# Attention with a second, transposed score product in place of transposed probabilities

## The reference

```python
q = _layer_norm(query, ln1_g, ln1_b)
qh = (q @ wq + bq).reshape(Bq, Sq, H, hd)
kh = (context @ wk + bk).reshape(Bq, Sc, H, hd)
vh = (context @ wv + bv).reshape(Bq, Sc, H, hd)
scores = jnp.einsum('bqhd,bkhd->bhqk', qh, kh) * scale
allowed = pos_in_block[None, :] <= jnp.arange(Sq)[:, None]
scores = jnp.where(allowed[None, None, :, :], scores, NEG_INF)
probs = jax.nn.softmax(scores, axis=-1)
o = jnp.einsum('bhqk,bkhd->bqhd', probs, vh).reshape(Bq, Sq, Dm)
x = query + o @ wo + bo
```

## Time and profile before

| | |
|---|---|
| Time, median of three executions | 2956.3 us |
| Profiled execution | 2956.78 us |
| Its span, mean granted TensorE clock | 2955.1 us, 0.989 |
| TensorE, VectorE, ScalarE, GpSimd busy in the span | 2786.7, 2033.4, 1654.5, 355.2 us |

### The profile page before, as it was taken

How to read it: one execution, slowest core, us unless ns; L and a number is a source line. 1 busy time by engine, 2 the same in 40 slices (tenths; PEclk the granted TensorE clock), 3 DMA queues, 4 the chain that set the end, 5 groups by cost and what they waited for, 6 DMA issues and landing times. The chain is left out here.

```text
span 2955.1 us, 65575 instructions
## 1 busy us (share of the span) xinstructions
PE 2786.7 (94%) x22056; PEld 2510.5 (85%) x22056; DVE 2033.4 (69%) x4884; ACT 1654.5 (56%) x4014; POOL 355.2 (12%) x364
## 2 busy tenths in 40 slices
PE   6999999999999999999984999999999899999999
PEld 4777777787777877777764999999999899999999
DVE  4766676667776677666756877877787766665566
ACT  3655666566655666566644565556556544444444
POOL 1211222112221122212210000000000000000000
PEclk9999999999999999999997999999999999999999
DMA  6666666667665676666634344334435343333442
GB/s 139 112 116 108 111 110 121 114 106 110 118 121 99 114 110 122 115 100 121 98 64 150 136 170 184 135 142 185 170 123 219 135 156 142 142 142 122 155 156 93
DMA packets 151738, 383.03 MB, mean 130 GB/s; under 512 B 12160, under 2 KB 16256, under 8 KB 143488
## 3 DMA queue, kind: packets, MB, share of 16 engines
q1 hardware_dynamic: 151680, 382.28, 52.8%
HBM read 172.51 MB, written 109.05 MB: 95 GB/s over the span
## 5 line engine op out<-in xcount | busy, mean ns | idle before, releaser
L711 ACT ACTIVATE sm<-sm,mins 128x128 f32<-128x128 f32 (+3 forms) x1024 | 571.6, 559 | 570.5 <-DVE mins L574 567.9
L574 DVE CUSTOM_DVE_ANT_0 sm<-bank_s,mask 128x128 f32<-128x128 f32 (+3 forms) x1024 | 480.6, 488 | 418.5 <-PE bank_s L425 416.2
L437 PE MATMUL bank_t<-ident,sm 128*128 128x128 f32 x2560 | 418.8, 278 | 73.8 <-DVE pT L520 37.4
L437 PEld LDWEIGHTS bank_t<-ident,sm 128*128 128x128 f32 x2560 | 299.6, 141 | 178.3 <-issue 58.3
L425 PE MATMUL bank_s<-stack 96*128 96x128 f32 (+3 forms) x1024 | 353.0, 386 | 8.4 <-DMA stack<-st_lo 7.9
L520 DVE COPY pT<-bank_t 128x384 f32<-128x384 f32 (+1 forms) x576 | 326.8, 567 | 1.3 <-PE bank_t L437 1.3
L1092 PE MATMUL bank_x<-b_hi,w_hi 128*128 128x256 f32 x1024 | 296.8, 290 | 26.9 <-ACT g L1515 21.6
L1092 PE MATMUL bank_x<-w_hi,a_hi 128*128 128x256 f32 x1024 | 291.2, 284 | 4.0 <-DVE a_lo L1212 4.0
L1093 PE MATMUL bank_x<-b_lo,w_hi 128*128 128x256 f32 x1024 | 291.1, 284 | 0.0
L1094 PE MATMUL bank_x<-b_hi,w_lo 128*128 128x256 f32 x1024 | 291.1, 284 | 0.0
L1094 PE MATMUL bank_x<-w_hi,a_lo 128*128 128x256 f32 x1024 | 290.9, 284 | 0.0
(11 more groups left out here) (178 smaller groups left out, 7389.4 us busy)
## 6 DMA issues: line engine op xcount, KB each, us to landing
stack<-st_hi SPq DMA_DIRECT2D x256, 256.0 KB, 6.1
xt<-in_x SPq DMA_DIRECT2D x32, 1024.0 KB, 5.1
stack<-st_lo SPq DMA_DIRECT2D x128, 256.0 KB, 7.3
xr<-x_scratch SPq DMA_DIRECT2D x32, 1024.0 KB, 5.6
b_scratch<-b_hi SPq DMA_DIRECT2D x16, 1792.0 KB, 10.0
b_scratch<-b_lo SPq DMA_DIRECT2D x16, 1792.0 KB, 13.7
b_hi<-b_scratch SPq DMA_DIRECT2D x16, 1792.0 KB, 7.5
b_lo<-b_scratch SPq DMA_DIRECT2D x16, 1792.0 KB, 11.2
```

Of the source, the lines that this page charges most:

```text
L437: mm = pe.transpose(bank_t[n % 2][:, P * c:P * c + P], sm[:, n % SLOTS_S, P * c:P * c + P], ident[:])
L574: op = V.tensor_tensor_reduce(sm[:, n % SLOTS_S, off:off + w], bank_s[n % BANKS_S][:, off:off + w], mask[:, 512 - w:512], 1.0, 0.0, ALU.ad ...
L711: op = A.activation(row, row, ACT.Exp, bias=mins[:, g % 2, c:c + 1], scale=-1.0, accum_out=sums[:, g % 2, c:c + 1])
```

## The change

Scores are computed twice. The first product is as before, but VectorE now writes its masked tile away as bf16 into `junk`, and only the minima are kept. Two-column products with the identity lay the minima of two heads as rows 96 and 97 of a PSUM bank (`minima_rows`); ScalarE copies them, negated and repeated for both heads, into rows 96 and 97 of `stack` (`minima_out`). Rows 96 and 97 of the key side hold ones and zeros that pick the head. The second product (`score_t`) then runs over 98 rows, with keys on partitions, and gives negated score less minimum, transposed. ScalarE takes the exponential from PSUM straight into `pT`, without a bias and without sums. GpSimd clears the masked half of the diagonal blocks (`mask_probs`) and adds the key tiles (`add_keys`). Job R becomes a product of those sums with ones, and VectorE takes the reciprocal of 128x512. `expand`, `r_copy`, `move_tile` and `p_transpose` are gone.

A group now has 20 steps: first scores in steps 0 to 11, second scores and exponentials of heads 0 and 1 in steps 9 to 11 and of heads 2 and 3 in steps 14 to 16, the V product in step 6 of the next group. BESIDE is laid out anew. ScalarE takes over the high part of the next context. In the start-up the order of a few operations on VectorE, ScalarE and TensorE is changed.

```diff
-SLOTS_S = 4
-LAG = 3
+SLOTS_S = 2
+BANKS_P = 2
+SCORES = [(r, qts) for p in (0, 2) for r, qts in
+          ((p, (0, 1)), (p + 1, (0, 1)), (p, (2,)), (p, (3,)), (p + 1, (2,)), (p + 1, (3,)))]
+MINIMA_AT = (7, 12)
+PROBS_AT = ((9, 10, 11), (14, 15, 16))
+PROBS = [(0, (0,)), (1, (0,)), (0, (1,)), (1, (1,)), (0, (2, 3)), (1, (2, 3))]
+KEY_AT = (0, 512, 896, 1152)
-    TG = 12
+    TG = 20
+    Q_AT, K_AT = {0: 4, 1: 4, 2: 4}, {3: 4, 4: 4, 5: 4}
     BESIDE = [
...
+        [("B", {0: 4}), ("Q1", Q_AT), ("K1", K_AT), ("R", {8: 8}), ("V1a", {9: 6, 10: 6, 11: 6, 12: 6}), ("O0", {14: 6, 15: 6}), ("O1", {16: 6, 17: 6})],
+        [("Q2", Q_AT), ("K2", K_AT), ("O2", {6: 6, 7: 6}), ("R", {8: 8}), ("V0b", {9: 6, 10: 6, 11: 6, 12: 6}), ("O3", {13: 6, 14: 6})],
+        [("Q3", Q_AT), ("K3", K_AT), ("V1b", {6: 8, 7: 8, 8: 8}), ("R", {8: 8}), ("X0", {15: 4}), ("X1", {16: 4}), ("X2", {17: 4}), ("X3", {18: 4})],
+        [("Q0", Q_AT), ("K0", K_AT), ("R", {8: 8}), ("V0a", {9: 6, 10: 6, 11: 6, 12: 6})],
     ]
+    PV_AT, RECIP_AT, O_PROD_AT, O_HIGH_AT, O_HIGH_LATE = 6, 9, 10, 11, 16
+    STATS_AT, NORMALISE_AT = (8, 9, 10, 11), (13, 13, 14, 14)
+    CONTEXT_AT = ((2, 9), (3, 1))
...
                 elif kind == "R":
-                    pe.wait_ge(rexp_ok, it.b * NG + g)
-                    for c in range(QT):
-                        mm = pe.transpose(bank[:, P * c:P * c + P],
-                                          rT[:, P * c:P * c + P], ident[:])
+                    pe.wait_ge(pre_ok, 2 * ADDS * (it.b * NG + g))
+                    for cols, src in ((slice(0, P), pT[:, :, 0:P]), (slice(P, 512), pre[:, :, :])):
+                        for h in range(4):
+                            mm = pe.matmul(bank[32 * h:32 * h + 32, cols], ones[:], src[:, h, :],
+                                           start=True, stop=True, skip_group_check=True)
...
+            def minima_rows(it, g, p):
+                n = PG * g + PG // 2 * p
+                pe.wait_ge(masked, it.b * TB + (SG * g + SG // 2 * (p + 1) + BANKS_S))
+                pe.wait_ge(scored_t_read, it.b * (NG * PG) + (n + 1))
+                for qt in range(QT):
+                    mm = pe.matmul(bank_p[n % BANKS_P][96:98, P * qt:P * qt + P], mins[:, g % 2, qt, 2 * p:2 * p + 2],
+                                   ident[:], start=True, stop=True, skip_group_check=True)
+                mm.then_inc(scored_t, 1)
+
+            def score_t(it, g, p, i):
+                n = PG * g + PG // 2 * p + 1 + i
+                pe.wait_ge(scored_t_read, it.b * (NG * PG) + (n + 1 + (i == 0)))
+                head, tiles = PROBS[i]
+                off = 0
+                for j in tiles:
+                    w = S - P * j
+                    mm = pe.matmul(bank_p[n % BANKS_P][:, off:off + w], stack[0:98, g % 2, 1, 2 * p + head, P * j:P * j + P],
+                                   stack[0:98, g % 2, 0, 2 * p + head, P * j:S], start=True, stop=True)
+                    off += w
+                mm.then_inc(scored_t, 1)
...
             def body(it):
                 for n, steps in enumerate(it.steps):
                     g, k = divmod(n, TG)
+                    if not it.tail and k < SG:
+                        score(it, g, k)
+                    for p in range(2):
+                        if not it.tail and k in PROBS_AT[p]:
+                            at = 2 * PROBS_AT[p].index(k)
+                            score_t(it, g, p, at)
+                            score_t(it, g, p, at + 1)
                     for job, i, j in steps:
                         dense_step(it, job, g, i, j)
+                    for p in range(2):
+                        if not it.tail and k == MINIMA_AT[p]:
+                            minima_rows(it, g, p)
+                    if k == PV_AT and not (it.first and g == 0):
+                        pv(it, g - 1)
...
+            def o_reciprocal(it, g):
+                bank = it.bank("R", g + 1)
+                dve.wait_ge(dense, it.done("R", g + 1))
+                dve.wait_ge(oT_done, it.b * NG + (g + 1))
+                V.reciprocal(rT[:], bank_d[bank][:]).then_inc(d_free[bank], 1)
...
+            def minima_out(it, g, p):
+                n = PG * g + PG // 2 * p
+                act.wait_ge(scored_t, it.b * (NG * PG) + (n + 1))
+                A.activation(stack[96:98, g % 2, 0, 2 * p:2 * p + 2, :],
+                             bank_p[n % BANKS_P][96:98, :].unsqueeze(1).to_broadcast([2, 2, S]),
+                             ACT.Identity, scale=-1.0).then_inc(scored_t_read, 1)
+
+            def exponential(it, g, p, i):
+                n = PG * g + PG // 2 * p + 1 + i
...
+                act.wait_ge(scored_t, it.b * (NG * PG) + (n + 1))
+                head, tiles = PROBS[i]
+                w = sum(S - P * j for j in tiles)
+                A.activation(pT[:, 2 * p + head, KEY_AT[tiles[0]]:KEY_AT[tiles[0]] + w], bank_p[n % BANKS_P][:, 0:w],
+                             ACT.Exp, scale=-1.0).then_inc(scored_t_read, 1)
...
+            def mask_probs(it, g, p):
+                n = PG * g + PG // 2 * p + 1
+                for j in range(QT):
...
+                    diagonal = pT[:, 2 * p:2 * p + 2, KEY_AT[j]:KEY_AT[j] + P]
+                    G_.affine_select(out=diagonal, in_=diagonal, compare_op=ALU.is_ge, fill=0.0, base=0,
+                                     pattern=[[0, 2], [1, P]], channel_multiplier=-1).then_inc(probs, 1)
+
+            def add_keys(it, g, p):
...
+                heads = slice(2 * p, 2 * p + 2)
+                G_.tensor_tensor(out=pre[:, heads, :], in0=pT[:, heads, P:S], in1=pT[:, heads, 512:896],
+                                 op=ALU.add).then_inc(pre_ok, 1)
+                for i, j in ((1, 2), (2, 3)):
+                    cols = slice(P * i, 384)
...
+                    G_.tensor_tensor(out=pre[:, heads, cols], in0=pre[:, heads, cols],
+                                     in1=pT[:, heads, KEY_AT[j]:KEY_AT[j] + S - P * j], op=ALU.add).then_inc(pre_ok, 1)
```

More of the change, by code:

```diff
@@ L627, in body @@
                     g, k = divmod(n, TG)
-                    if not it.tail:
-                        mask_and_max(it, n)
+                    if not it.tail and k < SG:
+                        mask_and_min(it, g, k)
                     for job, jg in it.ended(n):
@@ L632, in body @@
                             x_low(it, job, jg, it.b + 1)
[L633 to L634 removed]
                     beside_previous = g < NG and not (it.first and g == 0) and n < len(it.steps)
[L636 to L639 removed]
+                    if k == RECIP_AT and beside_previous:
+                        o_reciprocal(it, g - 1)
                     if k == O_PROD_AT and beside_previous:
@@ L741, in _ @@
             v_copy(pro, "V0a", 0)
+            act.wait_ge(consts, 1)
+            for par in range(2):
+                for p in range(2):
+                    A.copy(stack[96:98, par, 1, 2 * p:2 * p + 2, :],
+                           ident[96:98, 96:98].unsqueeze(2).to_broadcast([2, 2, S])).then_inc(chosen, 1)
             def body(it):
@@ L748, in body @@
                             x_high(it, job, jg)
-                    if not it.tail:
-                        exponential(it, n)
-                    if (n > LAG and not it.tail or n <= LAG and not it.first) and act_moves((n - LAG - 1) % TG):
-                        move_tile(act, A.copy, it, n - LAG - 1)
+                    for p in range(2):
+                        if not it.tail and k == MINIMA_AT[p]:
+                            minima_out(it, g, p)
+                        if not it.tail and k in PROBS_AT[p]:
+                            at = 2 * PROBS_AT[p].index(k)
+                            exponential(it, g, p, at)
+                            exponential(it, g, p, at + 1)
                     if not (it.first and g == 0):
-                        if k == R_AT:
-                            r_copy(it, g - 1)
                         if k == (O_HIGH_LATE if g == 1 else O_HIGH_AT):
                             o_high(it, g - 1)
+                    if not it.last and not it.tail:
+                        for half, at in enumerate(CONTEXT_AT):
+                            if (g, k) == at:
+                                for fb in (2 * half, 2 * half + 1):
+                                    context_high(it, it.b + 1, fb)
                     for job, jg in it.ended(n):
@@ L792, in o_low, with residual @@
+            def residual(b):
+                pool.wait_ge(res_in, b * 16 + 16)
+                for t in range(QT):
+                    G_.tensor_tensor(out=xt[:, t, :], in0=xt[:, t, :], in1=bo_row[:],
+                                     op=ALU.add).then_inc(res_ok, 1)
             def o_low(it, g):
```

261 lines of the change are left out of this document (106 added, 155 removed), and 4 rows, old and new, of the table BESIDE.

## The result

The changed kernel takes 3370.8 us (median, 3370.2 to 3371.8), the kernel before 2956.3 us beside it: a ratio of 1.141 [1.139, 1.143]. The forecast was 3207, with a range of 3020 to 3340. Sign and mechanism held, the size did not: +415 us where +251 were forecast.

The account below looks back on a forecast made before the run. TensorE was taken as the bound: 89.5 us of work plus 19.4 of waits made 108.9 a batch, +15.7, by 16 batches +251; last batch -6, tail +5. 2956.8 + 250 = 3207 us, range 3020 to 3340.

Parts of the forecast that it names:

- A: The forecast itself: whole kernel, TensorE's added work plus the new waits, 3207 us; chance 0.60.
- Rival C: TensorE runs its queue nearly dense once the copies go, waits 1.5 us a batch: faster, 2921 us; chance 0.08.
- B: Added latency hides in dense work, waits stay at 8.3 us a batch, only work grows: 3030 us; chance 0.15.
- Work, 89.5 us: TensorE's summed work in one batch of the attention stage at full clock: 89.5 us, 4.6 more than before.
- Step 12: Second pair's minima rows wait for VectorE's mask behind the reciprocal: nothing in groups 0, 1, 3; 1.9 us in group 2.
- Rival D: VectorE's 512-element reciprocal takes 4.2 us, delaying mask and minima rows 1.9 us in all four groups: 3329 us; chance 0.12.
- The clock at 1.00: TensorE in the attention stage: all 89.5 us of work a batch priced at full clock.
- rival E: TensorE's clock falls with gaps up to 3 us; 9 us of work a batch at half clock: 3351 us; chance 0.05.
- Steps 9 to 11, 14 to 16 and Q0: TensorE's waits for six exponentials twice a group, and Q0 of group 3 for X3: 3.7 + 6.4 + 2.6 us a batch.
- the old 8.3: Waits and gaps in the earlier kernel's 93.24 us batch, 8.3 us, forecast to go with the transpositions.
- Steps 12 to 14: Minima rows to ScalarE's copy to second score: 1.55 us without work beside in groups 0, 2, 3; 4.8 in all.
- GpSimd at nothing: GpSimd's adds (3.8 us) and four selects (2.6) per pair of heads cost TensorE no wait; doubled, up to 2 us a group.

Follow-up runs that it names:

- experiment 7: Changed kernel in 14-step groups, second-half minima, scores and exponentials beside the next group's Q and K; transposed minima, casts behind exponentials: 3093.6 us, 1.047.
- 11: The kernel of experiment 7 with 28 idle products a batch in its longest waits: 3060.0 us, 1.035.
- experiment 1: Changed kernel with a plain copy in place of VectorE's 128x512 reciprocal, the division left out: 3257.3 us, 1.102.
- experiment 2: Changed kernel with 57 idle 512-column products a batch put in TensorE's waits: 3296.2 us, 1.115.
- experiment 3: Changed kernel with GpSimd's adds in group 2 held until VectorE has normalised the next x: 3371.4 us, 1.141.
- experiment 9: The kernel of experiment 7 with statistics and O jobs a step earlier, inverse root ahead of GpSimd's adds, K0 earlier: 3103.8 us, 1.050.
- experiment 12: The kernel of experiment 7 with 15 idle products a batch and a copy in place of the reciprocal, division left out: 3023.4 us, 1.026.
- experiment 5: Changed kernel with minima laid as rows by four transpositions in place of four float32 products: 3322.2 us, 1.124.

## Why the prediction was wrong

The likeliest case was A. Of its steps:

- **Bound and sign: right.** TensorE is the bound, gets more work, and waits where there is no dense work beside. Rival C (faster) fell: the waits are 18 us a batch, not 1.5. B fell for the same reason; experiments 7 and 11 show how much of it would have been there with another order (a batch of 99.1).
- **Work, 89.5 us: 91.4.** The sums (0.94 forecast, 1.00 measured) and the V product (2.3) came as forecast. The minima rows did not: 0.27 us a product against 0.215, 8.6 us a batch instead of 6.9, which is 27 us in all. The price of the product was right, since the records of one set of four products start 0.109 us apart, 0.218 for the two of a product. What the sum left out is some 0.1 us at each end of a set: four products take 0.97 us from start to the next (649.42 to 650.39), and the one ahead of them is 0.09 longer. Two more terms were off by 2 us each and cancel: second scores at full clock take 1.39 us a pair of heads (0.47 + 0.51 + 0.41, 652.10 to 655.32), 11.1 a batch instead of 9.3, and first scores 3.0 a group (group 1), 12.0 a batch instead of 14.1.
- **Step 12, "nothing in groups 0, 1, 3", 1.9 us in group 2: this failed.** Measured 1.23 in each of the three and 3.48 in group 2, 7.2 a batch. The term that was mis-sized is the reciprocal: 2.3 us forecast from start to start, 3.27 measured (record 3.35). The mistake can be located in the earlier trace rows: I took 0.09 us of the 16-element pitch of 0.16 as fixed, by the neighbouring read. With 3.27 us for 512 elements and 0.16 for 16, it is 6.3 ns an element and some 0.06 fixed. A difference of two small numbers was carried on by a factor of 32. The queue behind it (masks, then minima rows) was counted correctly, and experiment 1 confirms it: with a short operation the wait stands in group 2 alone, 0.9 us. By the forecast's own rule 0.97 us more in four groups is 62 us, 3.9 a batch of the 5.3 by which these waits exceed the 1.9. The rest is TensorE, which reaches the rows earlier than walked: 5.2 us behind the end of the sums in group 0 where 5.5 was counted, 4.2 in group 2 where 4.85 was. Rival D had the right mechanism and too high a price: 8 passes at the mask's rate would be 8.1 ns an element, the Trainium skill's repeat count taken literally ("VectorE: DVE Perf Modes", "First, the fixed hardware budget"); the trace has 6.3.
- **The clock at 1.00: this failed too.** The sum priced all work at full clock, and rival E, at 0.05, had 9 us of work a batch at half clock. It was 13.38 + 6.67 us of busy records, which would be 10 us at full clock, close to E's 9. The row that I set against E, 25 of 35 us busy at 1.00, is an average over a stretch; it said nothing on how its idle time was divided. That stretch was 71% busy at 1.00, the changed kernel's batch is 87% busy at 0.89, so the share over a long stretch does not tell the clock. What stands around it is visible. The records date the fall at 594.7, just as the 3.48 us wait begins; TensorE had waited 0.29 and 0.74 us before it. Four more waits follow (1.11, 0.26, 1.07, 1.21) up to 611.0, and the clock is back at 615.2, after 4.2 us of Q0's products and scores without a wait. The second stretch, 635.7 to 642.5, is dense itself (6.7 us busy of 6.8); waits of 1.24, 1.11 and 0.45 us end 4, 2 and 1 us ahead of it. The Trainium skill warned of this ("TensorE: Matmul & The Clock Gate", "HAM oscillation"), and the trace agrees: the low clock comes back with each group 2. That idle time brings it is shown by experiment 2, which puts products in the waits and has 3.4 us at half clock instead of 27.3; it prices the clock at 75 us at least. Which of the waits it takes is open.
- **Steps 9 to 11, 14 to 16 and Q0, 3.7 + 6.4 + 2.6 us: over-sized.** Measured 3.2 us for exponentials and 1.2 ahead of Q0. In steps 9 to 11 of group 2, still at full clock, 0.29 + 0.74 us were lost where 2.8 stood in the sum; in its steps 14 to 16, at half clock, 0.26 + 1.07 for 3.3. That slower work of TensorE's own covers more of the round trips there is argued, not shown. With gaps, the waits sum to 18.1 against 19.4, so the total was nearly right by a short term and long ones. It is luck also because the forecast let all of the old 8.3 go with the transpositions, though the earlier trace rows has 5.1 of it ahead of them: the changed kernel has 3.0 us of gaps beside its 15.1 of idle time.
- **Steps 12 to 14, minima round trip, 1.55 us three times: right in kind.** 1.11 us of idle three times on the wait table, group 1 covered by O3, ScalarE's copy 1.02 us (1.1 forecast).
- **GpSimd at nothing: right for this kernel.** In a steady batch it is not named among TensorE's waits. The adds take 3.8 us a pair of heads, as forecast, the four selects 1.6 instead of 2.6. That it slows VectorE's normalisation was not foreseen; experiment 3 shows that it cost nothing. In experiment 9 GpSimd's place in the queue did cost 3.9 us.

The miss is 119.5 - 108.9 = 10.6 us a batch: work +1.9, clock +10.0, waits -1.3. Cases A, D and E stood as alternatives in the list, but they are not exclusive. A longer reciprocal lengthens a wait, and longer waits bring the clock down: A with 62 us for the reciprocal, 27 for minima rows and 75 for the clock comes to 3371 us, which is what was measured. That closeness is luck: experiment 2 gives only the lower end of the clock, and the over-sized and missing terms named above happen to cancel. The range ended at 3340 because D and E were each priced alone. It should have reached to their sum.

What stays open is the exact price of the clock alone (4.7 to 10.0 us a batch). The last 2.6% of experiment 12 have no single cause that was isolated. Not tried was the new order with a cheaper division, such as the old one on 128x16.

## What to carry to other kernels

Before trading a small operation for the same one on a large tile, find its price an element from two sizes; one short record here gave 4.4 ns for 6.3. An operation that stands ahead of a mask or a minimum in VectorE's queue can be paid for by TensorE. When a forecast adds waits of several us next to each other, price the work behind them at half clock too, and add the cases instead of listing them as alternatives. In this kernel the second stage of dependent work was better placed beside the next group's dense work than behind its own: of 415 us lost, moving it gave back 228 (experiment 7 less the 49 of experiment 5), a copy for the reciprocal 114 and holding the clock 75 (a run of its own each; the three overlap).

## What the runs showed of the hardware

- A reciprocal of 128x512 float32 on VectorE takes 3.35 us (3.27 from start to start), a copy of the same tile 0.69 (experiment 1).
- VectorE's float32 scalar operation from SBUF to SBUF takes 0.54 us alone and 0.98 to 2.04 while GpSimd adds or subtracts tiles of SBUF. The Trainium skill, "SBUF — State Buffer", "Who interferes with whom", has the two share a port pair that one holds for a whole instruction; the trace agrees in that each record of one batch's four ends 0.3 us after the GpSimd operation beside it, whose length goes from 0.73 to 1.82 us. What each loses, 0.44 to 1.50 us, is 0.3 to 0.5 less than that length; whether the whole operation is held back stays open.
- Two-column minima reach another quarter of the partitions by a transposition to partition 0 and ScalarE's copy to partition 96, whose time for 2x1024 did not change with the place (1.01 us from partition 0, 1.02 from 96).
- Idle time between TensorE's products costs clock, and products that are thrown away can pay: 57 of them a batch in the waits took the time at half clock from 27.3 to 3.4 us and 75 us off the kernel (experiment 2). Less work between the same waits went the other way: experiment 5 had transpositions for 32 products a batch, and 31.5 us at half clock.
- In one set, float32 products of two stationary and 128 moving columns start 0.218 us apart, in two records each, and transpositions of the same size 0.109, in one; the four products with what they add at both ends take 1.06 us.
